# New durations in the cost table of an order planner (two attention layers and an expert layer, one core)

## The reference

```python
x = x + conv_attention(group_norm(x))      # e1, e2, asm: 1x1 convolutions with PReLU; softmax(e1.T @ e2) @ asm
t = tokens(x)
t = t + additive_attention(layer_norm(t))  # score[i,j] = sum_a w2[a] * tanh(f[i,a] + g[j,a] + b1[a]); causal, exp, normalised
t = t + experts(layer_norm(t))             # softmax over the tokens, top 8 for each of 64 experts, two-layer FFN, scatter-add
```

## Time and profile before

| | |
|---|---|
| median of 3 runs | 5871.09 us (5862.58 to 5873.55) |
| the profiled execution's own time | 5872.08 us |
| its span | 5869.9 us |
| ACT busy, share of the span | 4930.1 us, 84% |
| of it the tanh of line 890 | 4151.5 us |
| PE busy, share of the span | 5078.5 us, 87% |
| DVE busy, share of the span | 2663.9 us, 45% |
| POOL busy, share of the span | 2001.5 us, 34% |
| mean granted clock of PE | 0.96 of full |

### The profile page before, as it was taken

The page is one execution under the profiler, slowest core; times in us unless marked ns, Lnnn a source line. Parts: engine busy times, 40 slices in busy tenths (PEclk is TensorE's granted clock), DMA queues, the critical chain, the costliest instruction groups (busy, mean ns, idle before and its releaser), DMA issues. The chain is left out here.

```text
span 5869.9 us, 71555 instructions
## 1 busy us (share of the span) xinstructions
PE 5078.5 (87%) x28567; PEld 1726.0 (29%) x28567; DVE 2663.9 (45%) x3558; ACT 4930.1 (84%) x4186; POOL 2001.5 (34%) x1643
## 2 busy tenths in 40 slices
PE   6999988889999978899999987889999987666657
PEld 2333332223333323222333333222333332111113
DVE  8853474433454466443453466443354454000132
ACT  0139969999989969999959969999978969999970
POOL 1474431125454431113464441112555451111110
PEclk8999999999999999999999999999999999888977
DMA  0000000000000010000000010000000010000028
GB/s 29 12 18 8 8 29 1 1 8 6 13 19 10 9 40 8 1 1 8 19 19 4 12 44 8 1 1 8 10 22 10 12 38 17 1 1 1 6 101 283
DMA packets 39418, 123.99 MB, mean 21 GB/s; under 512 B 4464, under 2 KB 5424, under 8 KB 31984
## 3 DMA queue, kind: packets, MB, share of 16 engines
q1 hardware_dynamic: 38272, 119.03, 6.1%
q10 hardware_dynamic: 816, 0.39, 0.0%
HBM read 89.85 MB, written 29.56 MB: 20 GB/s over the span
## 5 line engine op out<-in xcount | busy, mean ns | idle before, releaser
L890 ACT ACTIVATE tanh_slots<-query_part,key_part 128x2048 f32<-128x2048 f32 (+41 forms) x3072 | 4151.5, 1449 | 149.0 <-DVE key_part L1293 101.5
L946 PE MATMUL ps<-tanh_slots,packed 128*32 128x512 f32 (+2 forms) x18432 | 2080.7, 588 | 457.4 <-ACT tanh_slots L890 449.5
L846 POOL TENSOR_TENSOR context_and_exp_sums<-context_and_exp_sums,exp_scores 128x512 f32<-128x512 f32 (+3 forms) x544 | 632.8, 1185 | 2043.4 <-ACT exp_scores L902 1615.5
L946 PEld LDWEIGHTS ps<-tanh_slots,packed 128*32 128x32 f32 x18432 | 541.2, 113 | 1931.1 <-ACT tanh_slots L890 1094.3
L1369 DVE TENSOR_TENSOR _tokens_second_and_probs<-ps,e_and_minus_max 128x1024 f32<-128x1024 f32 x512 | 624.5, 1220 | 1059.5 <-PE ps L981 534.4
L859 POOL TENSOR_TENSOR conv_prob_sums<-conv_prob_sums,_tokens_second_and_probs 128x512 f32<-128x512 f32 x480 | 613.6, 1278 | 1151.6 <-ACT _tokens_second_and_probs L907 1146.5
L981 PE MATMUL ps<-_tokens_second_and_probs,asm_tokens 128*128 128x512 f32 x2048 | 995.6, 612 | 6.8 <-ACT _tokens_second_and_probs L907 6.8
L907 ACT ACTIVATE _tokens_second_and_probs<-_tokens_second_and_probs 128x1024 f32<-128x1024 f32 x512 | 549.2, 1073 | 454.2 <-DVE _tokens_second_and_probs L1369 454.1
L1345 DVE TENSOR_REDUCE row_max_parts<-ps 128x1 f32<-128x1024 f32 x512 | 608.4, 1220 | 452.6 <-PE ps L1060 440.6
L1205 DVE TENSOR_TENSOR context_and_exp_sums<-context_and_exp_sums,ps 128x512 f32<-128x512 f32 (+3 forms) x544 | 344.7, 638 | 717.6 <-PE ps L957 713.3
L861 POOL TENSOR_TENSOR conv_prob_sums<-conv_prob_sums,_tokens_second_and_probs 128x512 f32<-128x512 f32 x480 | 617.6, 1287 | 37.7
(11 more groups left out here) (156 smaller groups left out, 2062.4 us busy)
## 6 DMA issues: line engine op xcount, KB each, us to landing
y_scratch<-residual_chunks SPq DMA_DIRECT2D x64, 256.0 KB, 2.0
tanh_slots<-in_wg SPq DMA_DIRECT2D x16, 1024.0 KB, 10.5
residual_chunks<-y_scratch SPq DMA_DIRECT2D x63, 256.0 KB, 2.7
residual_chunks<-in_x SPq DMA_DIRECT2D x32, 256.0 KB, 2.8
e_and_minus_max<-p_scratch SPq DMA_DIRECT2D x32, 256.0 KB, 3.3
query_part<-in_x SPq DMA_DIRECT2D x4, 1024.0 KB, 6.0
normed_tokens_first<-in_x SPq DMA_DIRECT2D x4, 1024.0 KB, 8.5
p_scratch<-e_twice SPq DMA_DIRECT2D x4, 1024.0 KB, 6.8
```

Of the source, the lines that this page charges most:

```text
L846: pool.tensor_tensor(dst, dst, src, ALU.add).then_inc(s_ds, 1)
L890: nc.scalar.activation(S[:, 4 * (R % 2) + k, q:SUP], F[:, SUP * blk.s + q:SUP * blk.s + SUP], ACT.Tanh, bias=keypart(blk.b, kg, kg + 1)).t ...
L946: last = mm(PS[32 * k:32 * k + 32, t, off:CHUNK], w2k[:, g, :], S[:, 4 * (R % 2) + k, CHUNK * t + off:CHUNK * t + CHUNK], start=(g == 0), ...
```

## The change

Eleven numbers of the planner are changed, and no instruction, buffer, wait rule, dependency or rank. `HOP` goes from 0.08 to 0.12. The span of a full `T` goes from 0.1 + 1.706 = 1.806 to 0.19 + 1.706 = 1.896, that of a full `TR` from 0.89 to 0.91, of `E` from 0.57 to 0.62, of `K` from 0.35 to 0.3, of a full `C` on PE from 0.91 to 0.95, of `SM` from 1.25 to 1.2, of `EX` from 1.0 to 1.05, of `PS` from 2.6 to 2.7, of `M` on PE from 0.9 to 1.0 and on DVE from 1.25 to 1.18. `QK` stays at 1.1, `PV` at 1.9.

```diff
@@ -75,7 +75,7 @@
     FILL = {"F2a": "F2b", "FAa": "FAa", "L1": "L2", "L3": "L3", "L4": "L4", "L5": "L5", "G2": "G2", "G3": "G3",
             "Ea": "Ea", "Ev": "Ev", "M1": "M1", "g1": "g2", "g3": "g3", "g4": "g4", "g11": "g11"}
     FREE = {v: k for k, v in FILL.items()}
-    HOP = 0.08
+    HOP = 0.12
 
     def __init__(self):
         self.stages, self.ring = {}, {}
@@ -237,24 +237,24 @@
                     behind.append(("PE", "TR", R - 2, PER - 1))
                 if k == 0 and g == 0 and x.first:
                     behind.append(("DVE", "L5", x.b, PER * x.s + PER - 1))
-                prior_t = put("ACT", "T", (R, k), 0.1 + 0.833e-3 * (SUP - x.start(k, g)), behind, 4)
+                prior_t = put("ACT", "T", (R, k), 0.19 + 0.833e-3 * (SUP - x.start(k, g)), behind, 4)
             for t in x.ts:
                 w = (CHUNK - x.off(t)) / CHUNK
                 behind = [prior_t, prior_tr]
                 if g == 0 and t == x.ts[0]:
                     behind += [("DVE", "C", x.before[u], u) for u in x.ts if x.before[u] is not None]
-                prior_tr = put("PE", "TR", (R, t), 0.03 + 0.86 * w, behind, 2)
+                prior_tr = put("PE", "TR", (R, t), 0.02 + 0.89 * w, behind, 2)
     for i, (n, t) in enumerate(es):
         x = blocks[n]
         w = (CHUNK - x.off(t)) / CHUNK
         behind = [("PE", "TR", 4 * n + 3, t), prior_e]
         if i >= NEB:
             behind += [("PE", "C") + es[i - NEB], ("POOL", "D") + es[i - NEB]]
-        prior_e = put("ACT", "E", (n, t), 0.12 + 0.45 * w, behind, 1)
+        prior_e = put("ACT", "E", (n, t), 0.19 + 0.43 * w, behind, 1)
         done = [prior_e]
         if t == x.diag:
-            done.append(put("DVE", "K", (n, t), 0.35, [prior_e], 0))
-        put("PE", "C", (n, t), 0.05 + 0.86 * w, done, 3)
+            done.append(put("DVE", "K", (n, t), 0.3, [prior_e], 0))
+        put("PE", "C", (n, t), 0.07 + 0.88 * w, done, 3)
         behind = [("PE", "C", n, t)]
         if x.before[t] is not None:
             behind.append(("DVE", "C", x.before[t], t))
@@ -334,14 +334,14 @@
                 behind = [("PE", "QK", P), ("DVE", "SM", P - 1) if P else None, ("SP", "bc", b, c) if p == 0 else None]
                 if P >= 2:
                     behind += [("PE", "PV", P - 2), ("POOL", "PS", P - 2)]
-                put("DVE", "SM", (P,), 1.25, behind, 1)
-                put("ACT", "EX", (P,), 1.0, [("DVE", "SM", P), ("ACT", "EX", P - 1) if P else None], 2)
+                put("DVE", "SM", (P,), 1.2, behind, 1)
+                put("ACT", "EX", (P,), 1.05, [("DVE", "SM", P), ("ACT", "EX", P - 1) if P else None], 2)
                 behind = [("ACT", "EX", P)]
                 if P:
                     behind.append(("POOL", "PS", P - 1))
                 if p == 0 and cc >= 2:
                     behind.append(("PE", "F2a", (cc - 2) // NCH, (cc - 2) % NCH))
-                put("POOL", "PS", (P,), 2.6 if p else 1.3, behind, 3)
+                put("POOL", "PS", (P,), 2.7 if p else 1.3, behind, 3)
                 behind = [("ACT", "EX", P)]
                 if P:
                     behind.append(("PE", "PV", P - 1))
@@ -402,8 +402,8 @@
                 prior = put("DVE", kind, (b, ch), span, [("PE", kind, b, ch), prior], 4)
         for m in range(NPAIR):
             behind = [("DVE", "Ev", b, NCH - 1)] + max_free(b) if m == 0 else [("PE", "M", b, m - 1)]
-            put("PE", "M", (b, m), 0.9, behind + [("DVE", "M", b, m - 2) if m >= 2 else None], 4)
-            put("DVE", "M", (b, m), 1.25, [("PE", "M", b, m), ("DVE", "M", b, m - 1) if m else None], 4)
+            put("PE", "M", (b, m), 1.0, behind + [("DVE", "M", b, m - 2) if m >= 2 else None], 4)
+            put("DVE", "M", (b, m), 1.18, [("PE", "M", b, m), ("DVE", "M", b, m - 1) if m else None], 4)
         for i in range(parts(b)):
             put("DVE", "M0", (b, i), 0.3, [("DVE", "M", b, NPAIR // parts(b) * (i + 1) - 1)], 3)
             put("PE", "M1", (b, i), 0.2, [("DVE", "M0", b, i)], 3, ring=[7])
```

## The result

The changed kernel takes 5681.15 us (median of 4 runs, 5670.99 to 5688.11), the kernel before 5870.94 us (4 runs, 5862.58 to 5873.55). The ratio is 0.9678, 95% interval 0.9657 to 0.9699: 190 us or 3.2% faster. The forecast was 5814 us with a range of 5755 to 5880. The sign was right, and so was the main path (conv work moves from the gaps into the halves); the forecast size was less than a third of what came.

What follows compares the result with a forecast made beforehand. ACT's tanh sets the pace inside the halves and loses time in seven gaps (387 us). 31 + 17 + 10 = 58 us off 5872 gives 5814 us, range 5755 to 5880.

Steps and rivals of the forecast that it cites:

- (b, 0): First half of image b's second attention: 4 conv steps leave each of four gaps behind it, 31 us.
- (b, 1): Second half of image b: 3 steps leave each of three gaps behind it, 17 us; 1.7 more through M, 10 us.
- The room: PE's waits for tanh inside a half, 10.8 us, hold 5.3 more conv steps; mask waits (6.3 us) stay.
- The choice below the limits: Steps moved into halves: 4 and 3 taken, below the limits, as PE's helper work keeps its too short spans.
- A stretch put at nothing: Second halves: conv starts 12 us earlier, all from the M stage; no gain counted from gate and prep ahead.
- The M stage: Row maxima beside tanh: new M spans fit a fourth M into some rounds; up to 25 us, 12 taken.
- What a step is worth: A conv step moved from a gap into a half saves 2.97 - 1.06 = 1.91 us.
- The last half: Final half without conv beside it (853.2 us): one possible order at full width, -5 to +5 us, costed at nothing.
- More than that: Rival: PE's waits go whole, 7 steps per short gap, 8.6 behind each second half; 102 us, 5770; chance 0.2.
- Slower: Rival: inside the halves, early conv steps block ACT's tanh, 0.3 us for each EX; +47 us, 5919; chance 0.16.
- The gain is given back: Rival: PE already full, halves lengthen by what gaps lose; 0 to -12 us, 5866; chance 0.14.
- The row against HOP: Trace row in the M stage: PE to DVE took 0.17 us, not 0.12; 17 us in all without slack, not added.

Runs made afterwards that it cites:

- e1: The kernel before with only the fixed part of the tanh (T) span changed, 0.1 to 0.19; 5658.7 us.
- e6: The kernel before with the fixed part of T at 0.19 and M on DVE at 1.45, so the M stage keeps 46 rounds; 5739.4 us.
- e2: The changed kernel with the tanh (T) span put back, its fixed part at 0.1; 5860.1 us.
- e5: The kernel before with only the span of M on DVE changed, 1.25 to 1.15; 5825.5 us.
- e11: The changed kernel with both spans of M put back, 0.9 on PE and 1.25 on DVE; 5643.9 us.
- e12: The kernel before with only the fixed part of the tanh (T) span changed, 0.1 to 0.15; 5723.1 us.
- e4: The kernel before with only the fixed part of the tanh (T) span changed, 0.1 to 0.25, longer than the trace shows; 5710.1 us.
- e9: The changed kernel with HOP put back from 0.12 to 0.08; 5677.7 us.
- e7: The changed kernel with HOP and the spans of TR and C put back to their old values; 5618.9 us.
- e3: The kernel before with only the three ACT spans T, E and EX changed (0.19, 0.19 + 0.43 w, 1.05); 5630.6 us.

## Why the prediction was right or wrong

**What bounds the kernel, and what the change acts on: right.** ACT's tanh sets the pace in the halves, conv left over in the gaps costs time, and a longer tanh in the plan moves it in. e1 shows that this row alone does it. The measured spacing of 1.87 us and busy mean of 1.89 are what 0.19 stands for. The Trainium skill (ScalarE: Activation LUTs, What ACT_TABLE_LOAD costs) gives 280 ns + 0.833 ns per element for an instruction with a pointer as bias, and an overlap of 93 ns between two in a row. An estimate from these figures is 1.89 us for 2048 elements; the trace's 1.87 to 1.89 agrees. The old table had 0.1 us of the fixed part, about half of the 0.187 that the Trainium skill's figures leave.

**How many steps move: wrong, and the largest error.** I took 4 behind each (b, 0) and 3 + 1.7 behind each (b, 1), 30 in all. 63 moved: all 6 or 7 of each short gap, the one behind (0, 1) among them, and 14 or 15 of the 25 of each long one. Three steps of the reasoning failed.

- The room. I took PE's waits for tanh, 10.8 us, for all of it. In (2, 0) PE's idle time fell by 12.4 us, from 19.6 to 7.2, the waits for the mask with it.
- The choice below the limits. The plan's new room had come out as up to 11% more steps, and that was about right for (2, 0): 50 exps became 56. I went below it, to 4 and 3, for PE's helper work. Where conv alone could gain (e6, M stage held back) each long gap lost 8 steps, not 3 (some 2 of them by the next point).
- A stretch put at nothing. I had conv begin 12 us earlier in (b, 1), all of it from the M stage. In (2, 1) it begins 43 us earlier: the M stage gives 27 of them, and 16 come from the stretch of gate and prep ahead of it, 168 us instead of 184. At 7.0 us for a step that is 6 of the 14 steps. The 168 us come with the tanh row (e1 and e6 have 168, e2 and e5 183 and 185); what inside that stretch gives way was not looked into.

**The M stage: shorter, as I said, but in another way and by another row.** I had a fourth M come into some rounds, from the new spans of M. In the changed kernel no round has four. The stage is shorter because the rounds with the four C now hold three M where they held two. Played through on the host, the new plan shows how: behind a group of C the third M makes the next TR start 0.98 us after its tanh is ready, then 0.63, 0.29 and 0 us, so PE has no time left for a fourth M. My sum had that TR at 7.70 of the round, on time; the plan has rounds of 7.24 us there. The row that does it is the tanh: with it alone the stage is 322 us, without it 373 (e2), and the new spans of M on top of it cost (346 us, and 327 with them back, e11). The shorter stage also moved conv steps in: 80 of e1's 211 us need it. That its 27 us lie close to the "up to 25 us" of the prediction is luck.

**What a step is worth: too low.** I had 1.91 us, step against exp. The change gained 190 / 63 = 3.0 us for each, e12 148 / 49 = 3.0, e5 45 / 14 = 3.2, e6 131 / 50 = 2.6. The halves did get longer by what I had priced, 68 us for 63 steps at 1.06. But the gaps lost 250 us, not 63 x 2.97 = 187: the chain from the last PV to `L5`, which I held fixed, begins earlier with the steps, and part of it now runs beside the last tanh. 25 of these 63 us are the gap behind (1, 0), which had 43.0 us with 6 steps in it and closed whole; that of 26.0 us closed too, and the other short ones kept 18 to 21 us of their chain.

**The last half: costed at 0, -5 to +5; in the profile 15.8 us shorter.** That is more than I allowed, but it need not come from the order: two kernels with the same order there differ by as much, as the last section shows. What is surely the order's are the 183 us ahead of it, and the forecast was short by more than two thirds all the same.

**The rivals.** "More than that" had the right direction and stopped at 5770. Its bound of 7 steps in each short gap was reached; its 8.6 steps behind each (b, 1) were exceeded in the long ones. "Slower" did not come: ACT's waits inside (2, 1) for TR and SM are 18.5 us, about as before; they came in e4 only, with a planned tanh longer than the measured one. "The gain is given back" fell: PE's modelled 94% in (2, 0) rose to 98%, so a stretch that is shown that busy did have room.

**What stayed open.** The row against HOP (0.17 us from PE to DVE) was not tried; e9 shows only that 0.08 and 0.12 do not differ here. That measured spans for TR and C, or for M, cost 25 to 33 us a pair in the shared part is shown as to where: fewer steps inside, and a longer M stage with fewer fourth M. Why such a plan runs better on the chip is not. One reading that fits e7 and e4: a plan that has PE slightly too fast puts work ready for it ahead, and PE, at 99%, uses it; a plan that has ACT too slow makes ACT wait. That was argued, not shown.

## What to carry to other kernels

Where a planner's table lays out the order, compare its spans with start-to-start distances in the trace, first for the operation that occurs most often: 0.09 us on 3072 tanh decided 211 us, more than all other rows together. Then change the rows one by one on the chip; correcting every row that was measured was not the fastest, and the best versions here (e7 and e3, which cannot be told apart) beat the full correction by 1%. When you estimate what such a correction can move, look at all idle time of the receiving engine as room and not at one kind of wait, count the chain behind the last moved step with it, and ask of every stretch ahead of the moved work whether it gets shorter too.

## What the runs showed of the hardware that I had not expected

In the last half, once the gate's work is done, PE and ACT have only T, TR, E and C in their full-width blocks, and two blocks of the same work differ by 1.7 us at the same mean granted clock. Two blocks of the changed kernel, by stretch:

```profile
4794.43:4826.99 32.56, 23.12 (x138) 5.98 (x136) 3.16 (x5) 32.56 (x21) 4.81 (x4) 0.84 0.00 1
5024.10:5058.34 34.24, 22.60 (x137) 5.98 (x136) 2.75 (x5) 32.79 (x21) 5.10 (x4) 0.85 0.00 0
```

The granted clock is 0.84 and 0.85 of full in both, a mix of its two levels (1.2 and 2.4 GHz). In the chain of waits of that kernel the slower kind has a step that the faster one has not:

```profile
5016.40 5.34 PE ps L946 x32
5024.10 22.72 ACT tanh_slots L890 x13
5050.64 5.34 PE ps L946 x32
```

The four TR at the end of the block, for which ACT's E waits, take 5.34 us there, at a mean granted clock of 0.68; at a granted clock of 1.00 they take 3.64, as in the M stage. So it is not how long PE runs at the low level that costs, but whether that time falls on the one group of the block that ACT waits for. The last twelve full-width blocks of four traces (before, the change, e3, e7) bear it out: the 17 in which that group took 3.64 us are 32.55 to 32.58 us long, the 29 in which it took 5.2 to 5.3 are 33.9 to 34.3, and two with 6.5 are 35.1.

The order of the half alone does not set how the kinds are mixed. e3 and e7 have the same lists of PE, ACT, DVE and POOL in this half, position by position, and here is the half of e3, then of e7:

```profile
4594.20:5448.70 854.50, 586.31 (x3763) 172.65 (x3762) 176.10 (x355) 819.22 (x617) 134.45 (x115) 0.88 0.03 7
```

```profile
4596.30:5434.30 838.00, 580.84 (x3763) 170.01 (x3762) 175.87 (x355) 814.99 (x617) 133.67 (x115) 0.88 0.02 7
```

16.5 us apart, at the same mean granted clock: e3 has none of the fast kind among its twelve, e7 ten. The change has six and the kernel before one (837.7 against 853.5 us for the half). The runs of one kernel spread by 17 us (5670.99 to 5688.11) and those of before by as much (5857.8 to 5873.5 in the 13 beside e1). So up to some 16 us of a single comparison of profiles can be this; that it also makes the spread of the runs without a profile is likely, but was not shown.
